# Graph attention projections: the attention scores as extra columns of the layer's matrix

## The reference, cut to what matters

```python
h = (x @ W).reshape(n, heads, out_ch)
al_s = jnp.einsum('nhc,hc->nh', h, a_src)
al_d = jnp.einsum('nhc,hc->nh', h, a_dst)
```

| stage | input features | heads x width | columns of W | score columns |
|---|---|---|---|---|
| g0p | 256 (2 chunks of 128) | 4 x 64 | 256 | 8 |
| g1p | 256 (2 chunks) | 4 x 128 | 512 | 8 |
| g2p | 512 (4 chunks) | 4 x 128 | 512 | 8 |
| g3p | 512 (4 chunks) | 1 x 256 | 256 | 2 |

## Time and profile before

### The profile page before, as it was taken

One profiled execution on the slowest core, in us unless ns is written; L12 is line 12 of the kernel. 1 busy time (PEld: TensorE's weight loads), 2 busy tenths in 40 slices (PEclk: granted clock), 3 DMA queues, 4 the chain that ended last, 5 costly groups with the idle time before them and its releaser, 6 DMA issues. The chain is left out here.

```text
span 5671.2 us, 91348 instructions
## 1 busy us (share of the span) xinstructions
PE 4647.7 (82%) x33309; PEld 4126.5 (73%) x33309; DVE 3200.8 (56%) x2768; ACT 2791.6 (49%) x3666; POOL 1544.5 (27%) x1308
## 2 busy tenths in 40 slices
PE   1554777999998299948679999977999998897698
PEld 1443455999998178834379999956999997786454
DVE  4894212888886411125378888815888883542222
ACT  0662132777776022213067787714778773443222
POOL 3001000322222400040136666601666662011100
PEclk9776788999998599979789999988999998998767
DMA  2682013333431155530154434324443442553000
GB/s 46 110 136 39 3 75 78 101 100 89 101 91 44 45 181 174 182 105 8 41 143 102 108 97 107 87 61 122 100 109 97 108 98 68 138 131 78 14 11 23
DMA packets 231383, 503.04 MB, mean 89 GB/s; under 512 B 114188, under 2 KB 181912, under 8 KB 206299
## 3 DMA queue, kind: packets, MB, share of 16 engines
q1 hardware_dynamic: 206064, 468.25, 32.2%
q0 software_dynamic: 24720, 30.26, 2.5%
q10 hardware_dynamic: 288, 0.00, 0.0%
HBM read 412.64 MB, written 85.61 MB: 88 GB/s over the span
## 5 line engine op out<-in xcount | busy, mean ns | idle before, releaser
L1119 PE MATMUL g2a_pso<-HX,g2a_wt 125*125 125x129 f32 x5000 | 602.5, 274 | 5.4 <-ACT g2a_wt L1006 3.3
L1119 PE MATMUL g1a_pso<-HX,g1a_wt 125*125 125x129 f32 x5000 | 601.1, 274 | 4.1 <-ACT g1a_wt L1006 3.3
L1119 PE MATMUL g0a_pso<-HX,g0a_wt 125*125 125x65 f32 x5000 | 582.2, 270 | 4.0 <-ACT g0a_wt L1006 3.3
L1119 PEld LDWEIGHTS g2a_pso<-HX,g2a_wt 125*125 125x125 f32 x5000 | 576.2, 189 | 5.9 <-ACT g2a_wt L1006 3.5
L1119 PEld LDWEIGHTS g1a_pso<-HX,g1a_wt 125*125 125x125 f32 x5000 | 574.7, 188 | 4.5 <-ACT g1a_wt L1006 3.5
L1119 PEld LDWEIGHTS g0a_pso<-HX,g0a_wt 125*125 125x125 f32 x5000 | 571.9, 189 | 4.4 <-ACT g0a_wt L1006 3.4
L944 DVE SCALAR_TENSOR_TENSOR g2a_x<-g2a_als,g2a_cd,g2a_as 125x3125 f32<-125x3125 f32 x100 | 359.2, 3592 | 109.2 <-PE g2a_pst L1106 69.6
L944 DVE SCALAR_TENSOR_TENSOR g1a_x<-g1a_als,g1a_cd,g1a_as 125x3125 f32<-125x3125 f32 x100 | 358.2, 3582 | 107.9 <-PE g1a_pst L1106 69.1
L944 DVE SCALAR_TENSOR_TENSOR g0a_x<-g0a_als,g0a_cd,HX 125x3125 f32<-125x3125 f32 x100 | 347.8, 3478 | 119.1 <-PE g0a_pst L1106 80.0
L1006 ACT ACTIVATE g0a_wt<-g0a_pst 125x1000 f32<-125x1000 f32 (+1 forms) x300 | 312.0, 1040 | 181.6 <-PE g0a_pst L1106 181.6
L1006 ACT ACTIVATE g2a_wt<-g2a_pst 125x1000 f32<-125x1000 f32 (+1 forms) x300 | 312.2, 1041 | 168.9 <-PE g2a_pst L1106 168.7
(11 more groups left out here) (423 smaller groups left out, 8328.4 us busy)
## 6 DMA issues: line engine op xcount, KB each, us to landing
g0a_nl<-lowered SPq DMA_DIRECT2D x50, 1367.2 KB
g1a_nl<-lowered SPq DMA_DIRECT2D x50, 1367.2 KB
g2a_nl<-lowered SPq DMA_DIRECT2D x50, 1367.2 KB
lowered<-counts_nl SPq DMA_DIRECT2D x25, 1367.2 KB
g3a_nl<-lowered SPq DMA_DIRECT2D x25, 1367.2 KB
moe_wa<-in_L_ffn_W SPq DMA_DIRECT2D x32, 1024.0 KB
moe_wb<-in_L_ffn_W SPq DMA_DIRECT2D x32, 1024.0 KB
routed_rows<-mlp_zero SPq DMA_DIRECT2D x8, 1024.0 KB
```

What stands on the lines that cost most here:

```text
L1119: last = nc.tensor.matmul(pso[0:R, unit(q, 0, k) % 2, 0:F + 1], wt[:, side, j * R:(j + 1) * R], HX[:, a, q * HG + k % HG, :], start=(a == ...
```

## The change

The folded score vectors no longer have a matrix `wa` of their own. They are written as extra columns into `wt`, and one product gives both results, in one bank or two: a product of 264 columns in g0p (256 + 8), one of 258 in g3p (256 + 2), and in g1p and g2p, whose 512 columns fill a bank, two halves of 260 columns (256 + 4) in two banks. `PARTS` is the number of halves. VectorE reads the same two results from `ps` in the place of `psh` and `psa`. The matrix is loaded with one transfer for each chunk (KC of them) in the place of one.

```diff
+    PARTS = max(HF // 256, 1)
+    HP, WP = H // PARTS, HF // PARTS
+    SC = 2 * H // PARTS
...
-        wt = s.sb("w", [P, KC, HF])
+        wt = s.sb("w", [P, KC, PARTS, WP + SC])
         att, prod = s.sb("att", [P, 2, HF]), s.sb("prod", [P, 2, HF])
-        wa = s.sb("wa", [P, KC, 2 * H])
...
-        psh, psa = s.ps("psh", 3), s.ps("psa", 3)
+        ps = s.ps("ps", 3 * PARTS)
...
-        def scores(k):
-            return psa[0:R, RING3[k], 0:2 * H]
+        def banks(k):
+            return ps[0:R, RING3[k] * PARTS:(RING3[k] + 1) * PARTS, :]
...
-            sp.dma_start(wt[:], w.rearrange("(c p) n -> p c n", p=P)).then_inc(loaded, 16)
+            for c in range(KC):
+                sp.dma_start(wt[:, c, :, 0:WP], w[c * P:(c + 1) * P].rearrange("p (x n) -> p x n", x=PARTS)).then_inc(loaded, 16)
...
-                for c in range(KC):
-                    nc.tensor.matmul(psh[0:R, RING3[k], 0:HF], xs[:, k, c, :], wt[:, c, :], start=(c == 0), stop=(c == KC - 1))
-                for c in range(KC):
-                    last = nc.tensor.matmul(scores(k), xs[:, k, c, :], wa[:, c, :], start=(c == 0), stop=(c == KC - 1))
+                for x in range(PARTS):
+                    for c in range(KC):
+                        last = nc.tensor.matmul(banks(k)[:, x, 0:WP + SC], xs[:, k, c, :], wt[:, c, x, :], start=(c == 0), stop=(c == KC - 1))
                 last.then_inc(full, 1)
...
-                    nc.vector.tensor_tensor(prod[:, j, :], wt[:, c, :], att[:, j, :], ALU.mult)
+                    nc.vector.tensor_tensor(prod[:, j, :].rearrange("p (x n) -> p x n", x=PARTS), wt[:, c, :, 0:WP],
+                                            att[:, j, :].rearrange("p (x n) -> p x n", x=PARTS), ALU.mult)
                 nc.vector.drain()
-                last = nc.vector.tensor_reduce(wa[:, c, :], prod[:].rearrange("p j (h f) -> p (j h) f", h=H), AX_X, ALU.add)
+                last = nc.vector.tensor_reduce(wt[:, c, :, WP:WP + SC], prod[:].rearrange("p j (h f) -> p (j h) f", h=H), AX_X, ALU.add)
...
-                    nc.vector.tensor_tensor(HX[:, ds(t, 1), :, 0:F].rearrange("p o h f -> p (o h) f"),
-                                            psh[0:R, RING3[k], 0:HF].rearrange("p (h f) -> p h f", h=H),
-                                            bt[:].rearrange("p (h f) -> p h f", h=H), ALU.add).then_inc(h_free, 1)
-                    nc.vector.tensor_scalar(AL[:, 0:2 * H, ds(t, 1)], scores(k).unsqueeze(2), -1.0, None, ALU.mult).then_inc(al_free, 1)
+                    nc.vector.tensor_tensor(HX[:, ds(t, 1), :, 0:F].rearrange("p o (x h) f -> p (o x) h f", x=PARTS),
+                                            banks(k)[:, :, 0:WP].rearrange("p x (h f) -> p x h f", h=HP),
+                                            bt[:].rearrange("p (x h f) -> p x h f", x=PARTS, h=HP), ALU.add).then_inc(h_free, 1)
+                    nc.vector.tensor_scalar(AL[:, 0:2 * H, ds(t, 1)].rearrange("p (x n) o -> p x (n o)", x=PARTS), banks(k)[:, :, WP:WP + SC],
+                                            -1.0, None, ALU.mult).then_inc(al_free, 1)
```

More of the change, by code:

```diff
@@ L747, in multiply @@
                 pe.wait_ge(al_free, t + 1)
-                for c in range(KC):
-                    nc.tensor.matmul(psh[0:R, RING3[k], 0:HF], xs[:, k, c, :], wt[:, c, :], start=(c == 0), stop=(c == KC - 1))
-                for c in range(KC):
-                    last = nc.tensor.matmul(scores(k), xs[:, k, c, :], wa[:, c, :], start=(c == 0), stop=(c == KC - 1))
+                for x in range(PARTS):
+                    for c in range(KC):
+                        last = nc.tensor.matmul(banks(k)[:, x, 0:WP + SC], xs[:, k, c, :], wt[:, c, x, :], start=(c == 0), stop=(c == KC - 1))
                 last.then_inc(full, 1)
-            pe.wait_ge(loaded, 64)
+            pe.wait_ge(loaded, 16 * (KC + 3))
             if not from_rows:
@@ L773, in _ @@
         def _(dve):
-            dve.wait_ge(loaded, 64)
+            dve.wait_ge(loaded, 16 * (KC + 3))
             for c in range(KC):
                 for j in range(2):
-                    nc.vector.tensor_tensor(prod[:, j, :], wt[:, c, :], att[:, j, :], ALU.mult)
+                    nc.vector.tensor_tensor(prod[:, j, :].rearrange("p (x n) -> p x n", x=PARTS), wt[:, c, :, 0:WP],
+                                            att[:, j, :].rearrange("p (x n) -> p x n", x=PARTS), ALU.mult)
                 nc.vector.drain()
-                last = nc.vector.tensor_reduce(wa[:, c, :], prod[:].rearrange("p j (h f) -> p (j h) f", h=H), AX_X, ALU.add)
+                last = nc.vector.tensor_reduce(wt[:, c, :, WP:WP + SC], prod[:].rearrange("p j (h f) -> p (j h) f", h=H), AX_X, ALU.add)
                 if c < KC - 1:
```

## The result

| | median us | lowest to highest | runs |
|---|---|---|---|
| before | 5678.92 | 5666.77 to 5685.71 | 5 |
| changed | 5631.55 | 5614.08 to 5632.28 | 5 |

The ratio is 0.991 (95% interval 0.9888 to 0.9932), a gain of 47 us between the medians. The changed kernel was timed a second time, in four runs beside 23 of the one before. The ratio was 0.9896 (0.9874 to 0.9917), with medians of 5622.29 and 5679.63 us, 57 us apart. Against the forecast of 5618 us the first median is 14 us too high and the second 4; the first lies outside the forecast's own range (5606 to 5626 us) and inside the wide one, the second lies in both. The profiled execution of the changed kernel has a span of 5629.9 us, 41.3 less than that of before.

A forecast was written before the change was run, and what follows sets the result against it. Each projection was taken as bound by TensorE; savings of 11.4, 9.9, 18.8, 20.3 and 2.8 us less 2.8 for heads gave 60.4 off 5672.9, 5612.5, plus 6.0 to the median: 5618 us; own range 5606 to 5626, for all 5604 to 5634.

The forecast's parts named there:

- the wide one: The range for all cases, reaching over a late clock and slow loads: 5604 to 5634 us.
- What a narrow product costs: In the four projections each narrow product costs a weight load, 0.107 us, however few its columns.
- The rival by which narrow products are nearly free: The 600 narrow products of the four stages are worth little: gain 0 to 10 us, 5674 us; chance 0.03.
- The wait that replaces the work in g0p: In g0p tile t + 2 waits for VectorE's reads of tile t: 0.97 us a tile, against 0.89 for TensorE alone.
- the loop from lo: Stage lo's 1.83 us for two tiles, plus 0.03 for columns and the second read, gives g0p 1.95 us.
- The clock: g0p and g3p, with wide products only, rise after 3 us, not 9.3 and 8.6; g3p gains 2.8 us by it.
- The heads: Stage starts before the fold: 0.45 us lost in g0p and g1p each, 0.7 in g2p, 1.2 in g3p; together 2.8.
- the issue of one more transfer as a cost in itself: In each head, one more transfer ahead of the last load costs one issue, 0.37 to 0.50 us.
- The step on the size of the pieces: Matrix loads in smaller pieces were taken to cost nothing; by the skill's 138 GB/s the four would take 10.6 us longer.
- The sum: Savings in the four projections, with clock and heads: 11.4 + 9.9 + 18.8 + 20.3 + 2.8 - 2.8 = 60.4 us.
- The slower rival: The even stream of weights and products keeps the four stages' clock at 0.50: 146 us more, 5825 us; chance 0.02.

The follow-up runs named there:

- five banks: Changed kernel with five banks in place of three in g0p and g3p, five tiles between TensorE and VectorE in place of two; ratio 0.9898 to the kernel before.

## Why the prediction was right

**What a narrow product costs** was right to the hundredth, as was the pace of the wide ones. The periods of 1.756, 3.94 and 2.17 us came out as 1.76, 3.94 and 2.18. Padding and doubling show the cost apart from the change: 96 columns cost what 8 do, and one more product costs 0.108 us. The rival by which narrow products are nearly free fell with both. The Trainium skill's 25 ns, the least time between the starts of two matmuls ("TensorE: Matmul & The Clock Gate", section "Wait — 56ns, not 53.3ns?"), does not bind here. The Trainium skill gives a weight load as its columns divided by 1.2, in nanoseconds ("TensorE: Matmul & The Clock Gate", section "LDWEIGHTS (loading the stationary operand)"); for 125 columns I estimate 104 ns by it, and the trace agrees with 107.

**The wait that replaces the work in g0p** was right as a mechanism, and five banks removed it. Its size was a little off: two tiles take 2.03 us and not 1.95. I had taken the loop from lo by adding to its total. Counted through the changed kernel's own rows it is 1.41 us from the first load to the read (0.107, three steps of 0.223, 0.386 for the last product and 0.25 behind it), 0.51 for the reads and 0.11 to the next load. That is 1 us over the stage.

**The clock** was right in g0p: it rose 3 us after the first product where it had taken 9.3. The experiments support for g0p the reason that I had given without proof, that narrow products held it back: with them it took 9.5 and 12 us in two more profiles, with twice as many it did not rise in 85 us, and with their columns padded to 96 it rose after 4.5 us. In g3p the reason was wrong. The clock rose after 5.9 us, and after 5.0 in two profiles with the separate product, so the narrow products did not hold it there. Of the 2.8 us that I counted, 1.6 came, and only against the first profile of before, in which it rose after 9.0: that is luck. g2p lost 0.7 us the other way, rising after 4.5 us and not 3.1.

**The heads** were forecast at 2.8 us in sum, and were 2.7 (5.34, 8.21, 12.40 and 9.39 us against 5.45, 8.01, 10.82 and 8.34). That the sum agrees is luck, for the parts were not those that I gave: nothing in g0p, 0.2 in g1p, 1.6 in g2p and 1.0 in g3p, where the second profile of before has 0.8 us of it too. The step that failed is the issue of one more transfer as a cost in itself; with whole rows it cost nothing that shows in g0p to g2p. The step on the size of the pieces, which I took at nothing, failed in g2p, where cut rows in four transfers cost 1.5 us. By the estimate that the prediction drew from the Trainium skill ("DMA: Bandwidth & Descriptors", section "Measured (HBM→SBUF, 128 partitions, SWDGE, issued from GpSimd)"), 138 GB/s against 375, it would have been 4.8 us there for 1 MB. But the figure of 138 GB/s is given there for a transfer of 64 KB issued from GpSimd. The chunks here are of 128 and 256 KB and issued from SP, and no run has smaller ones.

**The sum** was 60.4 us. The four stages gave 59.5 - 2.7 = 56.8 between the first two profiles, and 55 between the second two (349.5 and 294.9 us from the first issues to the last reads, against 350.6 and 293.1). Of the 3.6 missing, g0p lost 1.4, g2p 0.8 and g3p 1.5 (57.9 us and not 56.4), as told above. The first comparison shows 47 us all the same, and the second 57. The difference fits g0's attention stage, 15 to 20 us longer in some profiles than in others, which no term of mine had; how it fell in the runs that weren't profiled isn't on record.

**The slower rival** did not come. A stage can stay at 0.50, the level of 1.2 GHz, from end to end, as g0p did with its score products doubled, but with narrow products and not with the even stream of wide ones that I had as the danger.

## What to carry to other kernels

A matmul whose columns take less time than its weight load cost the load in this kernel: 0.107 us, for 8 columns as for 96. Where two products share their stationary operand, the columns of the small one belong beside those of the large one, and two even products beat one of a full bank and a rest (1.76 us a tile against 2.15 in g1p).

After work is taken from the engine that bounds a loop, look for the ring that comes next, and count it from that loop's own rows. Here two tiles' distance became too short, and two more banks gave back TensorE's pace.

Read a local change in its own stages. Five runs against five were 10 us off, a fifth of the gain, most likely because of a stage that nobody had touched, while the windows of the four stages gave 57 and 55 us in two pairs of profiles.

## What the runs showed of the hardware

In g0p TensorE, busy 99% of the stage, stayed at 0.50 for 85 us when its products were four of 256 columns and eight of 8 columns in turn, and rose within 6 us when the eight had 96. With four and four of 8 columns it rose after 9.3, 9.5 and 12 us, and with the wide ones alone after 3 to 6. In g1p and g3p the doubled narrow products did not hold it: it rose after 3.4 and 3.5 us.

In a long stage of dense products (7471 of them) the clock differed between executions of kernels that are the same there: 825 to 830 us or 845.

From SP, a transfer of 128 partitions takes 0.42 us to issue with rows of 2 KB in one piece, and 0.60 us with each row in two pieces of 1 KB that are not adjacent in SBUF.
